# First-layer activations: their low parts subtracted on VectorE instead of on GpSimd

## The chip, the core and the metric

The kernel runs on one core of one Trainium2 chip. The metric is the device time of one launch in microseconds, from the inputs in HBM to the outputs in HBM. Arithmetic is in 32-bit floats. A matrix product of full precision is made of three products in the faster rounded format `fp32r`: each factor is split into a rounded high part and a low part (factor minus high part), and high·high, low·high and high·low are added up.

## The reference

Two blocks of a transformer follow each other, on 2 sequences of 1,024 tokens with 256 features and a context of 154 tokens each:

```
nx       = layernorm(x) * gamma + beta
evidence = softmax(nx Wq (ctx Wk)^T / 16) (ctx Wv)
combined = [nx, evidence, cond]                       # 768 features
probs    = softmax(combined router_W + router_b)      # 3 experts
h_e      = silu(combined e_w1[e] + e_b1[e])           # 512 columns for each of 3 experts
gate     = sigmoid(silu(combined gate_w1 + gate_b1) gate_w2 + gate_b2)
x        = x + gate * (sum_e probs_e (h_e e_w2[e] + e_b2[e]) out_w + out_b)
```

The second block normalizes `x` with a scale and shift from the condition, attends with 16 heads of 16 features to the (modulated) context, projects and adds to `x`.

## The kernel before

**Tiles and units.** The 2,048 tokens are 8 tiles `t` of 256. For each tile the "first layer" (the 256 columns of the gate and the 3 x 512 of the experts, 1,792 in all) is worked off in 7 units `u` of 256 columns. A unit goes through these steps, each a function of its engine's block:

- `za(t,u)` and `z(t,u)` on TensorE (PE in the profile; functions `hidden_first`, `hidden`): two halves of ten products each into one of two PSUM banks (`hidden_banks`).
- `z(t,u)` on ScalarE (ACT; `hidden`): tanh of the bank into the buffer `hidden` (TB).
- `z(t,u)` on VectorE (DVE; `hidden`): (tanh + 1) times the bank, in `hidden`. The PSUM bank is free after it.
- `h(t,u)` on ScalarE (`high`): the rounded copy, into `hidden_high` (SH).
- `h(t,u)` on GpSimd (POOL; `hidden`): `hidden` minus `hidden_high`, into `hidden_low` (SL).
- `p(t,u)` on TensorE (`second`): twelve products of `hidden_high` and `hidden_low` with the second layer's weights into `token_bank`; `evac` on VectorE adds the result, weighted with the expert's probability, to `expert_sum`.

TB, SH and SL have two buffers each, taken in turn, so the tanh of a unit waits until the low part of the unit before the last has been subtracted from TB, and both `h` steps wait for the `p` of the unit before the last.

**The second block of a tile** runs a tile later, between the units of the next one: `res`, `qn`, `shift`, `xhat`, `qx`, `qlow`, `query` make the queries; sixteen `most` steps (TensorE product, then a VectorE reduction over the 308 scores) find the maximum of each head, `row` transposes the maxima, and DMAs from the SP queue (function `row`) put them into the stack of queries; twelve `score` steps (product, exponential on ScalarE) and four `value` steps follow; and then, a tile later again, `raw` (ScalarE), `sum` (GpSimd), `dup`, `sums`, `out` (VectorE), `out` (ScalarE), `outl` (VectorE) and `proj`. `ln`, `norm`, `low`, `att`, `prob`, `route`, `logit` prepare the next tile's inputs and probabilities. `most`, `row` and `score` take three PSUM banks (`score_banks`) in turn: each product waits until the bank's user three before it has been read (`ring_free`).

**What sets the order.** Every engine works off a fixed list. `schedule()` gives each step a slot: tile `t` begins at slot 5 + 14 t, unit `u` at `step` x `u` after that, and each step's offset stands in `PLAN` or, for single tiles, in `PLAN_OF`; steps of one engine are then sorted by slot plus that engine's `DELAY`. The slots only make an order: at run time nothing waits but for semaphores (`wait_ge` with the count from `upto`). Some steps of the next tile have offsets below 14 counted from the tile before it (`ln` to `logit`). `PLAN` has two numbers for steps that the last tile takes in two parts; other tiles use the first one.

## Time and profile before

| | |
|---|---|
| device time, median of 3 runs | 438.0 us (437.63 to 439.25) |
| profiled execution, device time | 439.08 us |
| profiled execution, span on the core | 436.9 us |
| TensorE busy | 422.1 us |
| VectorE busy | 296.3 us |
| ScalarE busy | 223.6 us |
| GpSimd busy | 175.0 us |

The span runs from the first to the last recorded instruction; the device time of the same execution is 2.2 us longer. Busy is time in which an engine has an instruction in hand. A line of the profile names an instruction by its line number in the kernel, the engine, the operation, the output tile, and the input tiles. A helper that emits instructions for several steps has one line for them, as L1688 to L1690 (the three products of a split pair) and L1176 (`split_low`).

### The profile page before, as it was taken

To read this page: it belongs to the slowest core of one execution; us is meant where nothing else is said; L and a number is where in the kernel's file an instruction comes from. 1 tells how busy PE (TensorE), PEld (TensorE's weight loads), DVE (VectorE), ACT (ScalarE), POOL (GpSimd) and SP (SyncE) were. 2 spreads that over 40 slices of the span, in tenths; PEclk is the share of its full clock that TensorE was granted. 3 is DMA by queue.
4 is the path that set the end of the run, shared out by engine and by line. 5 is a ranking of instruction groups with operands and counts; after the bars stand their busy time and mean duration, and the time that the engine had idled before them with its cause. 6 is when DMAs were issued, how large, how long until landed. Compare 5 with 4: busy or idle time off the path is not lost.

```text
span 436.9 us, 9623 instructions
## 1 busy us (share of the span) xinstructions
PE 422.1 (97%) x3629; PEld 384.7 (88%) x3629; DVE 296.3 (68%) x748; ACT 223.6 (51%) x487; POOL 175.0 (40%) x184
## 2 busy tenths in 40 slices
PE   7899999999999999999999999999999899979996
PEld 6578999989998899889998899889988898868876
DVE  2785566674675696739863797389658755891797
ACT  2868643255347543764367246724672356326271
POOL 4545474553353526324523344344433632330020
PEclk9999999999999999999999999999999999998999
DMA  8786102531100210023000300030003021300301
GB/s 288 252 298 269 50 2 47 142 91 31 44 5 1 63 59 30 24 78 116 2 5 13 109 1 5 14 86 0 5 20 80 0 56 28 80 3 26 72 3 48
DMA packets 16837, 27.80 MB, mean 64 GB/s; under 512 B 3800, under 2 KB 9112, under 8 KB 16664
## 3 DMA queue, kind: packets, MB, share of 16 engines
q1 hardware_dynamic: 16664, 27.19, 21.2%
q8 instruction: 29, 0.48, 0.5%
q14 instruction: 16, 0.13, 0.1%
q10 hardware_dynamic: 128, 0.01, 0.0%
HBM read 15.94 MB, written 2.10 MB: 41 GB/s over the span
## 4 chain that ended last, share of the span: by engine, by line
PE 77%; DVE 15%; issue 3%; ACT 3%; DMA 1%; SPq 1%; ACTq 0%
PE hidden_banks L1688 7%; PE hidden_banks L1690 7%; PE hidden_banks L1689 7%; PE score_banks L1695 6%; PE score_banks L2060 5%; PE token_bank L1688 5%; PE token_bank L1689 5%; PE token_bank L1690 5%; PE score_banks L2030 4%; PE value_bank L2083 3%; PE value_bank L2086 3%; PE value_bank L1695 3%; DVE head_maxima L1463 3%; PE hidden_banks L1913 2%; DVE sums L1477 2%
## 5 line engine op out<-in xcount | busy, mean ns | idle before, releaser
L1620 POOL TENSOR_TENSOR hidden_low<-hidden,hidden_high 128x512 fp32r<-128x512 f32 x56 | 72.8, 1300 | 123.5 <-ACT hidden_high L1072 123.4
L1463 DVE TENSOR_REDUCE head_maxima<-score_banks 128x2 f32<-128x308 f32 x128 | 54.6, 473 | 17.1 <-PE score_banks L2030 15.0
L1688 PE MATMUL hidden_banks<-normed_high,hidden_w_high 128*128 128x256 f32 x224 | 64.2, 287 | 0.8 <-issue 0.8
L1689 PE MATMUL hidden_banks<-normed_high,hidden_w_low 128*128 128x256 f32 x224 | 62.5, 279 | 0.0
L1690 PE MATMUL hidden_banks<-normed_low,hidden_w_high 128*128 128x256 f32 x224 | 62.5, 279 | 0.0
L1132 ACT ACTIVATE exp_ring<-score_banks 128x512 f32<-128x512 f32 x96 | 52.6, 600 | 18.8 <-PE score_banks L2060 17.5
L1072 ACT CAST hidden_high<-hidden 128x512 fp32r<-128x512 f32 x56 | 34.8, 622 | 48.2 <-DVE hidden L1380 48.1
L1688 PE MATMUL token_bank<-expert_out_high,hidden_high 128*128 128x256 f32 x192 | 55.7, 290 | 0.0
L1064 ACT ACTIVATE hidden<-hidden_banks 128x512 f32<-128x512 f32 x56 | 33.3, 595 | 41.6 <-PE hidden_banks L1913 40.0
L1690 PE MATMUL token_bank<-expert_out_low,hidden_high 128*128 128x256 f32 x192 | 53.4, 278 | 0.0
L1689 PE MATMUL token_bank<-expert_out_high,hidden_low 128*128 128x256 f32 x192 | 53.4, 278 | 0.0
L1380 DVE SCALAR_TENSOR_TENSOR hidden<-hidden,hidden_banks 128x512 f32<-128x512 f32 x56 | 38.2, 683 | 18.5 <-ACT hidden L1064 18.3
L1688 PEld LDWEIGHTS hidden_banks<-normed_high,hidden_w_high 128*128 128x128 f32 x224 | 42.1, 188 | 2.1 <-issue 2.0
L1689 PEld LDWEIGHTS hidden_banks<-normed_high,hidden_w_low 128*128 128x128 f32 x224 | 42.3, 189 | 0.1
L1690 PEld LDWEIGHTS hidden_banks<-normed_low,hidden_w_high 128*128 128x128 f32 x224 | 42.0, 188 | 0.0
L1688 PEld LDWEIGHTS token_bank<-expert_out_high,hidden_high 128*128 128x128 f32 x192 | 36.2, 188 | 0.5 <-issue 0.2
L1689 PEld LDWEIGHTS token_bank<-expert_out_high,hidden_low 128*128 128x128 f32 x192 | 36.3, 189 | 0.2
L1690 PEld LDWEIGHTS token_bank<-expert_out_low,hidden_high 128*128 128x128 f32 x192 | 36.1, 188 | 0.0
L2030 PE MATMUL score_banks<-pair_keys,query_stack 96*128 96x308 f32 x112 | 29.4, 335 | 2.5 <-DVE head_maxima L1463 1.4
L1913 PE MATMUL hidden_banks<-probs_T_tail,context_w_tail 100*128 100x256 f32 x112 | 31.6, 282 | 0.0
L1689 PE MATMUL hidden_banks<-probs_T_high,context_w_low 128*128 128x256 f32 x112 | 31.2, 279 | 0.0
L1688 PE MATMUL hidden_banks<-probs_T_high,context_w_high 128*128 128x256 f32 x112 | 31.2, 279 | 0.0
(294 smaller groups left out, 1111.5 us busy)
## 6 DMA issues: line engine op xcount, KB each, us to landing
unit_weights<-units SPq DMA_DIRECT2D x7, 768.0 KB, 6.0
query_stack<-queries_high SPq DMA_DIRECT2D x56, 64.0 KB, 2.0
tokens<-x SPq DMA_DIRECT2D x8, 256.0 KB, 3.7
query_stack<-queries_low SPq DMA_DIRECT2D x28, 64.0 KB, 2.0
w_slice<-units SPq DMA_DIRECT2D x7, 256.0 KB, 3.0
out<-tokens SPq DMA_DIRECT2D x7, 256.0 KB, 2.4
w_T<-folds SPq DMA_DIRECT2D x6, 256.0 KB, 6.1
pair_keys<-keys_high SPq DMA_DIRECT2D x16, 77.0 KB
```

The lines of the kernel that those rows point to most:

```text
L1064: nc.scalar.activation(TB[:, ring(t, u), :], Z[:, hidden_bank(t, u), :], ACT.Tanh, scale=0.5).then_inc(scalar_z, 1)
L1072: nc.scalar.copy(SH[:, ring(t, u), :], TB[:, ring(t, u), :]).then_inc(scalar_h, 1)
L1132: nc.scalar.activation(E[:, w % ERING, :], S[:, ring_of[key][0], :], ACT.Exp).then_inc(scalar_score, 1)
L1380: v.scalar_tensor_tensor(out=TB[:, ring(t, u), :], in0=TB[:, ring(t, u), :], scalar=1.0, in1=Z[:, hidden_bank(t, u), :], op0=ALU.add, op1= ...
L1463: v.tensor_reduce(MX[:, s, first:first + step + 1:step], S[:, ring_of[key][0], 0:2 * CTX].rearrange("p (j n) -> p j n", j=2), AX.X, ALU.ma ...
L1620: nc.gpsimd.tensor_tensor(SL[:, ring(t, u), :], TB[:, ring(t, u), :], raw(SH[:, ring(t, u), :]), ALU.subtract).then_inc(gpsimd_h, 1)
L1688: mm(out_, lh, rh, start=start, stop=False, skip_group_check=skip)
L1689: mm(out_, ll, rh, start=False, stop=False, skip_group_check=skip)
L1690: return mm(out_, lh, rl, start=False, stop=stop, skip_group_check=skip)
L1695: last = mm(out_, l, r, start=(i == 0), stop=(i == len(pairs) - 1))
L1913: return mm(half, VWD[0:BROWS, b, c], PTD[0:BROWS, t % 2, :], start=False, stop=True)
L2030: mm(bank, QS[0:STACK, c, P * s:P * s + P], KS[b][0:STACK, c, :, :].rearrange("p j n -> p (j n)"), start=True, stop=True).then_inc(tensor_ ...
```

## The change

The `h` step that makes `hidden_low` moves from GpSimd's list to VectorE's, as a new function `hidden_low` that calls the existing helper `split_low` (a VectorE `tensor_tensor` with subtract). The tanh of ScalarE and `p` of TensorE wait on the new semaphore `vector_h` instead of `gpsimd_h`. All numbers of `PLAN`, `PLAN_OF`, `SETUP` and `DELAY`, from which the orders of the engines' lists come, are set anew. No other instruction is added or removed. The diff, cut to its core:

```diff
--- before.py
+++ after.py
@@ STEPS @@
         "logit": ["l", "s", "prob"],
         "z": ["s"],
+        "h": ["l"],
         "init": ["b"],
...
         "low": ["n"],
-        "h": ["l"],
         "qn": ["rstd"],
@@ DELAY, scalar @@
-        "logit": 1.7, "z": 0.81, "h": 0.3, "gate": 0.4, "qx": 0.4, "query": 0.1, "row": -0.4, "score": 0.2,
-        "out": 1.6, "xhat_last": -0.7, "qx_last": 0.2, "query_last": 0.2, "row_last": 0.5, "score_last": 0,
...
+        "logit": 1.2, "z": 0.9, "h": 0.4, "gate": 0.3, "qx": 0.9, "query": 0.15, "row": -0.2, "score": 0.15,
+        "out": 2.9, "xhat_last": -0.4, "qx_last": 0.3, "query_last": 0.1, "row_last": 0.3, "score_last": 0.1,
@@ DELAY, vector @@
-        "fold": -0.6, "vw": 0.6, "vt": 0.6, "w2": 0.6, "att": 0.2, "route": 0.4, "logit": 1.6, "z": 1, "evac": 0.5,
-        "query": 0, "most": 0.43, "row": 0.4, "proj": 2.5, "last": -0.2, "key": 0.6, "mod": 0.1, "bq": -0.3, "cb": 0,
...
+        "fold": -0.1, "vw": 0.6, "vt": 0.5, "w2": 0.7, "att": 0.1, "route": -0, "logit": 1.3, "z": 0.97, "evac": 0.5,
+        "query": 0.3, "most": 0.45, "row": 0.8, "proj": 2.3, "last": -0.6, "key": 0.4, "mod": -0.1, "bq": 0.7,
...
+        "outl_last": 0.3, "h": 0.6,
@@ DELAY, gpsimd @@
-        "h": 0.6, "ln": 0.86, "qn": -0.2, "low": 0.9, "keyn": 1.2, "split": 2.1,
+        "ln": -0.4, "qn": 0.7, "low": 0.8, "keyn": 3, "split": 1.4,
@@ DELAY, sync @@
-        "query": 13.4, "row": -3.6, "proj": 1.5, "last": -2.1, "key": -0.9, "place": 11.3, "query_last": 3.7,
-        "row_last": -3.6, "stack_last": 1.9,
+        "query": 23.4, "row": -0.7, "proj": 2.7, "last": -3.8, "key": -2.1, "place": 13.3, "query_last": 8.6,
+        "row_last": -12.6, "stack_last": 0.9,
@@ PLAN @@
-    "dup": (37.2, 49.2), "za": -0.4, "step": 1.99, "z": 0.38, "h": 1.5, "p": 3.3, "again": -6.4, "vw": -38.8,
-    "ln": 0.2, "norm": 1.6, "low": 6.6, "att": 7.9, "prob": 9.1, "route": 12.3, "logit": 14.4, "res": 17.4,
-    "qn": 18.4, "shift": 18.5, "xhat": 19.3, "qx": 19.54, "qlow": 20.1, "query": 20.7,
-    "most": (22.11, 22.29, 23.89, 24.92, 26.01, 26.34, 27.35, 28.05), "row": (29.2, 30.6),
...
-    "out": (38.34, 56.69), "outl": (43.37, 97.85), "proj": 43.6, "last": (16, 59.3), "reload": 45.3, "init": 5.2,
+    "dup": (36.83, 44.29), "za": -0.12, "step": 2, "z": 0.45, "h": 1.7, "p": 3.2, "again": -3, "vw": -44, "ln": 6.8,
+    "norm": 1.3, "low": 5.5, "att": 7.7, "prob": 12.7, "route": 12.6, "logit": 14.2, "res": 16.4, "qn": 17.38,
+    "shift": 18, "xhat": 18.42, "qx": 18.7, "qlow": 19.5, "query": 20.4,
+    "most": (22.27, 22.35, 22.87, 23.42, 25.81, 26.78, 27.42, 28.01), "row": (28.65, 36.67),
...
+    "out": (15.7, 77.9), "outl": (42.9, 80.4), "proj": 44.2, "last": (6.5, 80.9), "reload": 55.9, "init": 6.9,
@@ PLAN_OF: it had entries for tiles 0, 1, 3, 5, 6 and 7, and has them for all eight; tiles 2 and 3 @@
+    2: {
+        "norm": 1.6, "value": (34.15, 34.2, 36.28, 36.3), "prob": 8.6, "ln": -0.3, "logit": 16.1, "qx": 18.5,
+        "score": (31.5, 31.7, 32.6, 32.7, 33, 33.3, 34, 34.4, 34.5, 35, 35.3, 35.5), "sums": (37.7, 46),
+        "out": (39.1, 57.1),
+    },
     3: {
-        "vw": 0.9,
+        "proj": 44.3, "logit": 13.8, "qx": 18.4, "ln": -3.8,
+        "score": (32.68, 32.8, 32.9, 33.6, 33.89, 34.23, 34.35, 34.49, 35.23, 35.29, 35.46, 35.56), "vw": 0.94,
+        "value": (35.1, 35.2, 36, 36.3), "norm": 1.8, "query": 20.1, "att": 7.5, "out": (38.5, 58.1), "prob": 7.8,
+        "sums": (37.8, 50.1), "qlow": 19.1, "dup": (37.1, 42.8),
     },
@@ PLAN_OF of tile 6, from which its ln step is placed @@
-        "raw": (34.4, 34.5), "proj": 47.7, "most": (21.9, 22, 24.8, 25.8, 26.5, 27.3, 27.4, 28), "ln": 0.9,
...
+        "most": (21.8, 21.9, 25.1, 25.7, 26.4, 27.1, 27.3, 28.2), "ln": 0.2,
...
@@ scalar, hidden @@
-                    act.wait_ge(gpsimd_h, upto(gpsimd_h, ("h", (g - 2) // NU, (g - 2) % NU), "l"))
+                    act.wait_ge(vector_h, upto(vector_h, ("h", (g - 2) // NU, (g - 2) % NU), "l"))
@@ vector @@
+            def hidden_low(key):
+                t, u = key[1:]
+                g = NU * t + u
+                dve.wait_ge(scalar_h, upto(scalar_h, key, "h"))
+                if g >= 2:
+                    dve.wait_ge(tensor_p, upto(tensor_p, ("p", (g - 2) // NU, (g - 2) % NU), "p"))
+                split_low(SL[:, ring(t, u), :], TB[:, ring(t, u), :], SH[:, ring(t, u), :]).then_inc(vector_h, 1)
@@ gpsimd @@
-            def hidden(key):
-
-                t, u = key[1:]
-                g = NU * t + u
-                pool.wait_ge(scalar_h, upto(scalar_h, key, "h"))
-                if g >= 2:
-                    pool.wait_ge(tensor_p, upto(tensor_p, ("p", (g - 2) // NU, (g - 2) % NU), "p"))
-                nc.gpsimd.tensor_tensor(SL[:, ring(t, u), :], TB[:, ring(t, u), :], raw(SH[:, ring(t, u), :]),
-                                        ALU.subtract).then_inc(gpsimd_h, 1)
@@ tensor, second @@
                 pe.wait_ge(scalar_h, upto(scalar_h, ("h", t, u), "h"))
-                pe.wait_ge(gpsimd_h, upto(gpsimd_h, ("h", t, u), "l"))
+                pe.wait_ge(vector_h, upto(vector_h, ("h", t, u), "l"))
```

## Rows read from the trace of the kernel before

**Rows 1.** The page: busy time of each engine, and the chain that ended last by engine.
```profile
PE 422.1 (97%) x3629; PEld 384.7 (88%) x3629; DVE 296.3 (68%) x748; ACT 223.6 (51%) x487; POOL 175.0 (40%) x184
...
PE 77%; DVE 15%; issue 3%; ACT 3%; DMA 1%; SPq 1%; ACTq 0%
```

**Rows 2.** Waits of TensorE: what waited for whom, us in total, times, longest.
```profile
PE score_banks L2060 <- DMA query_stack<-max_low: 1.7, 1, 1.7
PE score_banks L2030 <- DVE head_maxima L1463: 1.4, 6, 0.3
...
PE score_banks L2030 <- DMA query_stack<-queries_high: 0.9, 1, 0.9
...
PE hidden_banks L1688 <- issue: 0.8, 1, 0.8
...
PE head_bank L1980 <- ACT x_hat L1089: 0.6, 1, 0.6
```

**Rows 3.** Windows from the third maximum on, for six tiles: length, busy time by engine.
```profile
150.04:164.72 14.68, 14.55 (x121) 14.27 (x120) 14.52 (x35) 5.36 (x10) 5.86 (x7) 1.00 0.21 60
196.82:211.50 14.68, 14.68 (x114) 14.27 (x113) 14.13 (x33) 6.51 (x13) 5.04 (x6) 1.00 0.28 84
243.59:258.27 14.68, 14.48 (x120) 14.20 (x119) 14.55 (x34) 5.36 (x10) 5.84 (x7) 1.00 0.20 56
286.97:301.65 14.68, 14.46 (x121) 14.14 (x120) 14.55 (x34) 5.33 (x10) 5.85 (x7) 1.00 0.15 36
330.24:344.92 14.68, 13.69 (x112) 13.17 (x111) 12.90 (x31) 5.43 (x10) 9.27 (x10) 1.00 0.14 35
374.00:388.68 14.68, 13.43 (x104) 12.27 (x103) 14.35 (x32) 4.99 (x9) 6.69 (x9) 1.00 0.13 31
```

**Rows 4.** Groups of instructions: busy us in all, mean ns of one, idle before them.
```profile
L1620 POOL TENSOR_TENSOR hidden_low<-hidden,hidden_high 128x512 fp32r<-128x512 f32 x56 | 72.8, 1300 | 123.5 <-ACT hidden_high L1072 123.4
...
L1429 DVE TENSOR_TENSOR tokens<-expert_sum,tokens 128x512 f32<-128x512 f32 x8 | 5.5, 692 | 0.3
```

**Rows 5.** Timeline of VectorE: start, duration, instruction.
```profile
248.67 0.45 DVE L1496 STREAM_SHUFFLE sums_spread<-sums 128x256 f32<-128x256 f32 x1
...
251.96 0.86 DVE L1463 TENSOR_REDUCE head_maxima<-score_banks 128x2 f32<-128x308 f32 x2
252.73 0.87 DVE L1417 SCALAR_TENSOR_TENSOR expert_sum<-token_bank,router_probs,expert_sum 128x256 f32<-128x256 f32 x2
...
254.29 0.41 DVE L1176 TENSOR_TENSOR probs_T_low<-head_bank,probs_T_high 128x256 fp32r<-128x256 f32 x1
...
258.27 0.74 DVE L1166 BATCH_NORM_STATS2 stats<-tokens 128x6 f32<-128x256 f32 x2
...
259.41 1.28 DVE L1506 SCALAR_TENSOR_TENSOR outs_low<-outs_high,constants,outs_twice 128x1024 fp32r<-128x1024 f32 x1
...
267.42 0.69 DVE L1429 TENSOR_TENSOR tokens<-expert_sum,tokens 128x512 f32<-128x512 f32 x1
268.03 0.68 DVE L1518 TENSOR_TENSOR tokens<-tokens,value_bank 128x512 f32<-128x512 f32 x1
```

**Rows 6.** Timeline of TensorE in the same stretch: `p(4,4)`, a wait, `p(4,5)`, `row(3,0)`.
```profile
249.38 0.28 PE L1688 MATMUL token_bank<-expert_out_high,hidden_high 128*128 128x256 f32 x1
...
252.49 0.41 PE L2030 MATMUL score_banks<-pair_keys,query_stack 96*128 96x308 f32 x1 [0.20 <-DVE head_maxima L1463]
...
254.29 0.28 PE L1688 MATMUL token_bank<-expert_out_high,hidden_high 128*128 128x256 f32 x1
...
259.23 0.39 PE L2039 MATMUL score_banks<-constants,head_maxima 128*16 128x128 f32 x2
```

**Rows 7.** Timeline: four VectorE adds alone, the same beside a GpSimd step, that step.
```profile
227.25 1.80 DVE L1397 SCALAR_TENSOR_TENSOR expert_sum<-expert_bias,router_probs,expert_sum 128x256 f32<-128x256 f32 x4
...
361.00 2.82 DVE L1397 SCALAR_TENSOR_TENSOR expert_sum<-expert_bias,router_probs,expert_sum 128x256 f32<-128x256 f32 x4
...
361.27 1.35 POOL L1620 TENSOR_TENSOR hidden_low<-hidden,hidden_high 128x512 fp32r<-128x512 f32 x1 [2.46 <-ACT hidden_high L1072]
```

More of the change, by code:

```diff
@@ L310 @@
-    7: {
-        "route": 13.2, "most": (19.2, 19.2, 19.3, 19.4, 19.4, 19.6, 20.3, 20.5), "init": 5.6, "sums": (28.4, 36),
-        "za": -0.73, "score": (22.06, 22.59, 22.73, 23.07, 23.16, 23.16, 23.63, 23.73, 24.03, 24.23, 24.34, 24.54),
-        "outl": (33.4, 33.8), "row": (19.96, 21.53), "h": 1.2, "p": 3.5, "last": (39.5, 39.7), "query": 18.06,
-        "xhat": 17.7, "ln": 0.5, "value": (23.2, 23.5, 24.7, 25.8), "proj": 38, "logit": 14.9, "out": (27.3, 33.2),
-        "raw": (23.1, 28.7), "qlow": 18, "qx": 17.62, "dup": (24.9, 28.7), "step": 1.96,
+        "row": (28.6, 36.8),
@@ new lines @@
+        "score": (31.23, 32.12, 32.26, 32.36, 32.85, 33.42, 33.77, 34.21, 34.46, 35.13, 35.28, 36.12),
+        "value": (32.94, 34.35, 36.27, 36.29), "qx": 18.5, "out": (38.5, 64.2), "sum": (34.8, 38), "h": 1.36,
+        "most": (22.27, 22.79, 24.33, 24.75, 25.7, 26.97, 27.6, 28.07), "sums": (37.6, 47.2),
+    },
+    1: {
+        "norm": 1, "p": 3.5, "value": (33.1, 34, 36.2, 36.2), "query": 20.8, "sum": (34.4, 37.3), "prob": 8.4,
+        "ln": -0.1, "score": (31.6, 32.5, 32.6, 32.9, 33.6, 33.6, 34, 34.2, 34.7, 35.4, 35.6, 36.1),
+        "out": (39.3, 63.5), "low": 6.2, "most": (22.28, 22.31, 23.14, 23.27, 25.87, 26.74, 27.32, 28.07),
+        "qlow": 19.3, "logit": 13.4, "qn": 17.7, "sums": (37.7, 47.1),
+    },
@@ new lines @@
+    4: {
+        "prob": 10.2, "most": (22.27, 22.4, 22.9, 23.48, 25.94, 26.78, 27.43, 28.01),
+        "value": (33.97, 34.81, 36.11, 36.12), "sums": (37.3, 48.9), "out": (38.5, 59.6), "query": 20.9,
+        "score": (31.36, 31.82, 32.08, 33.42, 33.42, 33.83, 34.3, 34.52, 34.82, 35.35, 35.54, 35.62), "ln": -0.5,
+        "dup": (36.9, 44.6),
+    },
+    5: {
+        "proj": 43.87, "shift": 18.4, "ln": 0.45, "query": 20.8,
+        "most": (22.4, 22.4, 22.9, 23.4, 26, 26.8, 27.5, 28.1), "value": (32.53, 33.96, 35.56, 35.9), "qlow": 20.7,
+        "prob": 8.29, "score": (31.87, 31.87, 31.94, 32.53, 33.17, 33.5, 34.12, 34.13, 34.17, 35.22, 35.28, 35.44),
+        "out": (38.6, 58.5), "qx": 19.4, "sums": (37.5, 47.4),
+    },
@@ new lines @@
+    6: {
+        "sums": (37.1, 47.1), "prob": 8.5, "stack": (17.1, 18, 23.6, 25.7), "raw": (34.5, 35.2), "logit": 14.97,
+        "out": (37.2, 60.7), "value": (31.9, 31.9, 35.1, 35.6), "att": 7.5, "query": 20.2,
+        "most": (21.8, 21.9, 25.1, 25.7, 26.4, 27.1, 27.3, 28.2), "ln": 0.2,
+        "score": (30.6, 30.7, 30.8, 31.3, 31.4, 31.7, 31.9, 32.1, 32.6, 32.6, 32.8, 32.9), "init": 6.2,
+    },
+    7: {
+        "step": 1.97, "outl": (31.9, 34.9), "xhat": 17.4, "value": (23.4, 23.4, 25.4, 26), "ln": 1.4,
+        "raw": (22.9, 26.6), "h": 1.5, "low": 6.8, "init": 5.9, "query": 18.3, "norm": 3.3, "p": 3.4,
+        "most": (18.9, 19, 19.1, 19.2, 19.3, 19.4, 19.4, 19.6), "prob": 8.7, "qx": 17.7, "dup": (25.5, 28.7),
+        "out": (27.45, 32.07), "res": 16.94,
+        "score": (22.1, 22.2, 22.3, 22.6, 22.8, 23.3, 23.3, 23.5, 23.5, 23.7, 23.9, 24.3), "logit": 14,
+        "sums": (30.5, 33.3), "qlow": 17.4, "row": (20.6, 21.7), "last": (40, 41.5), "proj": 39.6,
```

50 lines of the change are left out of this document (22 added, 28 removed).

## The prediction

> **What bounds the kernel now.** I read the page first, then TensorE's waits, then the windows and timelines of one tile. TensorE has work in hand for 422 of 436.9 us [rows 1]: the reader should see that it is full nearly everywhere, so a change can gain only what TensorE waits, and loses whatever it makes TensorE wait. The named waits from the first `most` on are few [rows 2]: 1.7 us for the DMA of the last row of maxima, 1.4 us for the reductions of `most` in six pieces, 0.9 us for the queries, 0.8 and 0.6 us for single events, 5.4 us together. The rest of the 436.9 - 422.1 = 14.8 us in which it is idle lies in small pieces, in the setup and at the very end.
>
> A mean load of 68% on VectorE hides where it matters. The chain is 15% VectorE [rows 1]. The windows show where it is full: from the third `most` of a tile on, VectorE also makes the division and spreading of the tile before (`dup`, `sums`, `out`). In windows of 14.68 us from that point VectorE is busy for 14.52, 14.13, 14.55, 14.55, 12.90 and 14.35 us [rows 3]. In five of six tiles it is as full as TensorE. GpSimd is busy for 5.0 to 9.3 us in the same windows. Nothing in TensorE's waits names the low parts of the activations: GpSimd stands 123 us waiting to be given them [rows 4]. The step moves from the engine with room to the one that shares the path there.
>
> **The price of one step.** On GpSimd it takes 1300 ns. VectorE has no `hidden_low` before; the same operation on the same shape from SBUF is L1429, 692 ns [rows 4]. Its successor starts 0.61 us after it (268.03 - 267.42) [rows 5], and this is what a step costs a full queue. 56 x 0.61 = 34 us of VectorE's queue (by durations 56 x 0.692 = 39, so 296 to 335 us busy), and 73 us less for GpSimd. The step issues no DMA. The latency of a unit's low part falls by 1300 - 692 = 0.6 us where neither engine queues; TensorE doesn't wait for it now, so I credit that with nothing. Two other things hang on the step: ScalarE's tanh of the unit after the next, and everything behind it in VectorE's list. It waits for ScalarE's rounded copy, so VectorE stands if it is placed too early. The slots put it 0.88 after VectorE's `z` (1.7 + 0.6 against 0.45 + 0.97), some 2.7 us at 14 slots to the 286.97 - 243.59 = 43.4 us of a tile [rows 3], so that wait costs nothing.
>
> **One stretch worked out: the maxima of tile 3.** The new slots (5 + 14 t + offset + delay) give VectorE from `most(3,2)` on: two `most`, `dup`, two `most`, `z(4,4)`, `sums`, two `most`, **`h(4,4)`**, `out`, `z(4,5)`, `evac`, two `most`, **`h(4,5)`**, `route`, two `most`, `z(4,6)`, two `most`, **`ln(6)`**, **`h(4,6)`**, the last two `most`. Before, the same steps stood there without the bold ones (`ln(6)` came after the last `most`), and a 0.08 us reciprocal that now comes earlier. TensorE's list has the same sets of work between the milestones as before, so its times carry over.
>
> - `p(4,4)`: before, all but the third pair of `most` was done at 248.67; that pair costs 252.73 - 251.96 = 0.77. So `h(4,4)` starts at 248.67 + 0.77 - 0.08 = 249.36 and ends at 250.05. TensorE is there at 249.38 [rows 5, 6]: 0.7 us late.
> - `p(4,5)`: VectorE had finished this set at 254.29. Now 254.29 - 0.08 + 0.61 = 254.82, and `h(4,5)` ends at 255.51. TensorE is there at 254.29 - 0.20 (the wait at 252.49 goes, since the pairs of `most` move forward) = 254.09: 1.4 us late.
> - `row(3,0)`: the last `most` ended at 258.27. Added are 3 x 0.61 = 1.83 for `h` and 259.41 - 258.27 = 1.14 for `ln(6)`, less 0.08: 2.89, so 261.16. TensorE is there at 259.23 - 0.20 = 259.03: 2.1 us late.
>
> These lags are measured from the same schedule, so they don't add: TensorE loses 2.1 us here, against 0.2 before. Net 1.9 us.
>
> **The other five stretches.** All get three `h` steps, 1.83 - 0.08 = 1.75 us; only the one above gets `ln` too. Against this stand VectorE's idle time in the window [rows 3] and the lead of the last `most` over `row`, 259.23 - 258.27 = 0.96 us in tile 3 [rows 5, 6], which I take for all. Tiles 1 and 4: idle 0.16 and 0.13, so 1.75 - 0.96 - 0.15 = 0.6 by `row`, and up to the 1.4 of `p(4,5)` by the middle of the stretch; I take 1.0 each. Tile 2: idle 0.55, so 0.2 to 1.4, taken 0.8. Tile 5: idle 1.78, because TensorE came late itself, taken 0.2. Tile 6: here TensorE has little else to do (13.43 of 14.68 us) and the next thing behind VectorE is the 1.7 us DMA wait, so all of it, 1.8. With 1.9 for tile 3 the sum is 1.0 + 0.8 + 1.9 + 1.0 + 0.2 + 1.8 = 6.7 us. Bounds: nothing, if the new order lets VectorE begin earlier by as much; 6 x 2.1 = 12.6 us, if each is like tile 3's.
>
> **The rest.** Of the other waits, 0.9 + 0.8 + 0.6 = 2.3 us [rows 2], the new slots change the surroundings of all; half, 1.2 us, is credited, with 0 and 2.3 as bounds. Setup and tail: VectorE's steps in the tail stand in nearly the same order, and the last `h` lies before them; in the setup the slots of all steps move a little, and nothing in the rows names this step there; 0, with 1 us either way. `init` moves from before `qlow` to before `query`, into idle time of VectorE: 0. `sum` on GpSimd moves later by its slot, but by order only behind `prob`: 0.
>
> Sum against the profiled execution: 439.1 (436.9 of span and 2.2 around it) + 6.7 - 1.2 = 444.6. That execution is 1.1 us above the median of the runs, so 443.5.
>
> **A rule against the step.** An add of four on VectorE, both inputs in SBUF, takes 1.80 us alone and 2.82 us where a GpSimd step that reads SBUF stands beside it [rows 7]; the difference is 1.02 us. The Trainium skill, page "SBUF — State Buffer", section on its two separate sides, says that GpSimd and a VectorE operation with two SBUF inputs take one shared port pair as an exclusive lock for a whole instruction; by that rule, the trace agrees. What it would do here is rival 2.
>
> **Rivals.**
>
> 1. *The order absorbs it (no change).* The new slots pull four pairs of `most` ahead of `sums` and `out`, so the reductions no longer wait behind them; for it speaks that VectorE idles 436.9 - 296.3 = 141 us of the span elsewhere. Against it: the total before `row` is what counts, and it grows. With losses of 0.3 us a stretch: 439.1 + 1.8 - 1.2 = 439.7, so 438.6 beside the median.
> 2. *The lock makes it worse.* Each new step has two SBUF inputs. GpSimd without `hidden_low` still works for 175 - 73 = 102 us, 23% of the span, so some 13 of 56 steps meet one; at up to 1.02 us each in the full stretches (18 steps, 4 meetings) that is 4 us more: 447.5. Against it: its largest user of the port, `hidden_low` itself, has gone from GpSimd.
> 3. *Faster.* GpSimd's step was in the way of `low`, `prob`, `norm` and `sum`, and the freer lists let the new order close TensorE's waits. All 5.4 us of the waits in rows 2 gone gives 438.0 - 5.4 = 432.6; half, the likelier, 435.3. It decides if the load added per stretch falls below the lead of 0.96 us, as by `out` or `ln` done outside it. Against: in rows 3 VectorE has no such room, and these waits name other engines.
>
> **How the numbers follow.** Forecast 0.47, rival 2 0.10, rival 1 0.18, rival 3 0.25. Differences within 0.5% (2.2 us) are about what a measurement of this kernel can tell from no change: slower 0.57, same 0.18, faster 0.25. The range reaches to rival 3's half way less the setup's 1 us, 434.5, and past rival 2's to 448; the forecast's own range is 440.5 to 447.
>
> **What would show it.** `hidden_low` on VectorE at 690 to 700 ns x56 and VectorE near 335 us; GpSimd near 102 us. TensorE's products of `p` (L1688, `token_bank`) waiting for VectorE's `hidden_low` in several tiles, 0.5 to 1.5 us each, and `row` (L2039) waiting for the last reduction; TensorE's busy time unchanged near 422 us, the span longer by the waits alone. I am wrong if the six windows show VectorE full while TensorE doesn't wait (the work before `row` has been cut elsewhere), or if the gain comes from the last tile's wait for the maxima.

## The result, and the profile after

The changed kernel takes 448.4 us in the median (446.76 to 449.32, four runs); the kernel before, run beside it on the same chip, 438.6 us. The ratio is 1.021, with a 95% interval of 1.018 to 1.025. The forecast was 443.5 us and "slower"; the direction is right, the loss is 8 to 10 us instead of 5.5, and the median lies 0.4 us above the upper end of the range. The profiled execution took 446.76 us with a span of 445.0, against 439.08 and 436.9 before: 8.1 us in the spans, and the steps below are read from these.

First the page of the changed kernel: busy time by engine, and the chain that ended last.

```profile
PE 425.7 (96%) x3629; PEld 386.8 (87%) x3629; DVE 324.4 (73%) x804; ACT 222.7 (50%) x487; POOL 104.2 (23%) x128
...
PE 60%; DVE 21%; SPq 6%; issue 5%; ACT 4%; DMA 2%; POOL 0%; POOLq 0%; ACTq 0%; DVEq 0%
```

Against [rows 1] VectorE has 28 us more, GpSimd 71 us less, and VectorE's share of the chain has gone from 15% to 21%. Then the groups of instructions with the moved step, and beside it a step of GpSimd that will matter (busy us in all, mean ns of one, idle before them).

```profile
L1200 DVE TENSOR_TENSOR hidden_low<-hidden,hidden_high 128x512 fp32r<-128x512 f32 x56 | 39.6, 708 | 11.3 <-ACT hidden_high L1096 11.0
...
L1643 POOL TENSOR_TENSOR normed_low<-normed,normed_high 128x512 fp32r<-128x512 f32 x8 | 10.3, 1289 | 40.0 <-ACT normed_high L1052 40.0
```

TensorE's waits (us in total, times, longest), which answer to [rows 2]:

```profile
PE score_banks L2052 <- DVE head_maxima L1495: 4.2, 9, 1.0
PE score_banks L2061 <- DVE head_maxima L1495: 2.5, 5, 1.4
PE token_bank L1710 <- DVE hidden_low L1200: 1.6, 3, 0.5
...
PE score_banks L2052 <- DMA query_stack<-queries_high: 1.1, 2, 0.8
```

Waits for the maxima have grown from 1.4 to 4.2 us, the `row` transposition waits for the last reduction five times, and `p` waits for the low part three times. All of these but two waits of 0.3 us stand in the stretches from a tile's third maximum to its `row`. The windows of 14.68 us from about the third maximum on, as in [rows 3], for tiles 1 to 4 (length, TensorE, its weight loads, VectorE, ScalarE, GpSimd):

```profile
151.43:166.11 14.68, 13.65 (x112) 13.25 (x111) 14.55 (x33) 5.16 (x10) 1.48 (x2) 1.00 0.20 58
200.70:215.38 14.68, 14.68 (x113) 14.21 (x113) 14.55 (x35) 4.69 (x10) 2.48 (x4) 1.00 0.24 63
246.86:261.54 14.68, 13.54 (x110) 13.00 (x109) 14.55 (x33) 5.15 (x10) 2.00 (x3) 1.00 0.14 35
292.60:307.28 14.68, 13.56 (x112) 13.14 (x110) 14.55 (x33) 5.12 (x10) 1.48 (x2) 1.00 0.10 23
```

VectorE is full in all four, as it nearly was before, and in three of them TensorE no longer is: in tile 3, 13.54 against 14.48 us busy, and 110 products against 120 in the same time. That TensorE has lost, and waits for VectorE, is the sign that VectorE has become the bound of this stretch; its own 14.55 us of 14.68 would not show it, since it had nearly as much before. In tiles 5 and 6 the same windows have VectorE at 14.55 and 14.00 us and TensorE at 13.65 and 12.58, against [rows 3] 12.90 and 14.35, 13.69 and 13.43. VectorE's timeline of tile 3, the stretch that the prediction worked out (start, duration), beside [rows 5]:

```profile
246.86 0.86 DVE L1495 TENSOR_REDUCE head_maxima<-score_banks 128x2 f32<-128x308 f32 x2 [0.28 <-PE score_banks L2052]
...
252.62 0.70 DVE L1200 TENSOR_TENSOR hidden_low<-hidden,hidden_high 128x512 fp32r<-128x512 f32 x1
...
258.06 0.69 DVE L1200 TENSOR_TENSOR hidden_low<-hidden,hidden_high 128x512 fp32r<-128x512 f32 x1
258.66 0.42 DVE L1200 TENSOR_TENSOR probs_T_low<-head_bank,probs_T_high 128x256 fp32r<-128x256 f32 x1
...
261.83 0.74 DVE L1190 BATCH_NORM_STATS2 stats<-tokens 128x6 f32<-128x256 f32 x2
...
262.97 0.69 DVE L1200 TENSOR_TENSOR hidden_low<-hidden,hidden_high 128x512 fp32r<-128x512 f32 x1
263.58 0.86 DVE L1495 TENSOR_REDUCE head_maxima<-score_banks 128x2 f32<-128x308 f32 x2
```

And TensorE's, beside [rows 6]: `p(4,4)`, `p(4,5)`, `row(3,0)`, with the wait ahead of each in brackets.

```profile
253.46 0.35 PE L1710 MATMUL token_bank<-expert_out_high,hidden_high 128*128 128x256 f32 x1 [0.52 <-DVE hidden_low L1200]
...
258.85 0.36 PE L1710 MATMUL token_bank<-expert_out_high,hidden_high 128*128 128x256 f32 x1 [0.62 <-issue]
...
264.50 0.39 PE L2061 MATMUL score_banks<-constants,head_maxima 128*16 128x128 f32 x2 [0.42 <-DVE head_maxima L1495]
```

The low part of 252.62 ends at 253.32 and `p` starts at 253.46; the next ends at 258.75 and `p` starts at 258.85, though the trace puts that wait down to "issue"; the last reduction runs until 264.44 and `row` starts at 264.50. From the start of the third maximum to `row` it is 264.50 - 246.86 = 17.6 us, before it was 259.23 - 243.59 = 15.6.

**The whole span in these pieces.** I cut the timeline of each kernel in this way: until the first tile's `row`; the six stretches from the third maximum to `row` of tiles 1 to 6; the six pieces between, from one `row` to the next third maximum; and from the last of these `row` products to the end.

| us, profiled execution | to first `row` | six stretches (each) | six pieces between | after the last | span |
|---|---|---|---|---|---|
| before | 124.1 | 97.0 (16.6 17.9 15.6 15.6 17.2 14.2) | 167.0 | 48.8 | 436.9 |
| after | 124.3 | 103.5 (17.6 18.7 17.6 16.5 16.7 16.3) | 169.8 | 47.4 | 445.0 |

The stretches lost 6.5 us, where the prediction's sum was 6.7; the pieces between lost 2.8 us that it did not have; the end came out 1.4 us shorter.

The pieces do not hold quite the same work in both kernels. Counted by products, TensorE does 748 in the six stretches before and 739 after, and 1,544 and 1,559 in the pieces between. Ten products have moved from just ahead of a `row` to behind it (and one of `z` the other way): six router products (`logit`) in tile 4, and four of `w_slice` in tile 1, which took from 165.65 to 166.60, so 0.95 us. TensorE in tile 4, before:

```profile
302.00 0.17 PE L1900 MATMUL head_bank<-router_context,probs_T_high 128*128 128x8 f32 x1
...
302.58 0.39 PE L2039 MATMUL score_banks<-constants,head_maxima 128*16 128x128 f32 x2
```

and after:

```profile
309.06 0.39 PE L2061 MATMUL score_banks<-constants,head_maxima 128*16 128x128 f32 x2 [0.17 <-DVE head_maxima L1495]
309.20 0.25 PE L1922 MATMUL head_bank<-router_context,probs_T_high 128*128 128x8 f32 x1
```

Six more router products have moved out of the first piece in the same way. With 0.58, 0.95 and 0.59 us put back where they stood, the loss for the same work is 0.8 us up to the first `row`, 8.0 in the stretches (2.0 in tile 1 and 1.5 in tile 4 instead of 1.1 and 0.9), 0.7 in the pieces between, and -1.4 at the end.

### The profile page after: what moved, and what is told of

The parts are those of the page before. It is cut to its first block, busy times and chain, and to the rows that moved or that the text cites. A ratio compares the mean times of both kernels' runs of the same rounds, so it can differ in the third digit from the quotient of the medians.

```text
span 445.0 us, 9623 instructions
## 1 busy us (share of the span) xinstructions
PE 425.7 (96%) x3629; PEld 386.8 (87%) x3629; DVE 324.4 (73%) x804; ACT 222.7 (50%) x487; POOL 104.2 (23%) x128
## 4 chain that ended last, share of the span: by engine, by line
PE 60%; DVE 21%; SPq 6%; issue 5%; ACT 4%; DMA 2%; POOL 0%; POOLq 0%; ACTq 0%; DVEq 0%
DVE head_maxima L1495 6%; PE hidden_banks L1710 5%; PE hidden_banks L1712 5%; PE hidden_banks L1711 5%; PE score_banks L2082 4%; PE score_banks L1717 4%; PE token_bank L1710 4%; PE token_bank L1712 4%; PE token_bank L1711 4%; PE value_bank L2105 3%; PE value_bank L2108 3%; PE score_banks L2052 2%; DVE hidden_low L1200 2%; DVE hidden L1404 2%; SPq L880 2%
## 5 line engine op out<-in xcount | busy, mean ns | idle before, releaser
L1710 PE MATMUL hidden_banks<-normed_high,hidden_w_high 128*128 128x256 f32 x224 | 65.3, 291 | 0.0
L1710 PE MATMUL token_bank<-expert_out_high,hidden_high 128*128 128x256 f32 x192 | 56.6, 295 | 2.6 <-DVE hidden_low L1200 1.6
L1200 DVE TENSOR_TENSOR hidden_low<-hidden,hidden_high 128x512 fp32r<-128x512 f32 x56 | 39.6, 708 | 11.3 <-ACT hidden_high L1096 11.0
L1566 POOL TENSOR_TENSOR rstd<-mean_var,minus_half 128x2 f32<-128x2 f32 x18 | 13.9, 772 | 135.4 <-DVE mean_var L1195 135.4
L1712 PE MATMUL hidden_banks<-probs_T_low,context_w_high 128*128 128x256 f32 x112 | 31.3, 279 | 0.0
```

The source lines that it names most:

```text
L1200: return v.tensor_tensor(dst, full, raw(high), ALU.subtract)
L1710: mm(out_, lh, rh, start=start, stop=False, skip_group_check=skip)
L1712: return mm(out_, lh, rl, start=False, stop=stop, skip_group_check=skip)
```

## The experiments

The kernel before ran beside each and had medians of 438.8 to 439.2 us. "Times" are medians; the pieces are those of the table above.

### 1. The order alone, and the move alone

The first kernel has the changed kernel's slots, but subtracts on GpSimd (delay 0.6, and `sum` at its slots of before). The second has the slots of before, but subtracts on VectorE (delay 0.6). Both kernels have the function `h` on both engines, and one new function says which of them takes a unit:

```diff
+def low_engine(t, u):
+    return "gpsimd"        # first kernel, lists of after
+    return "vector"        # second kernel, lists of before
```

> All slots of the change, but the low parts stay on GpSimd (and its two sums keep their old slots). Theory (the load on VectorE between the third maximum and row costs TensorE its time): about as fast as the kernel before, ratio 0.995 to 1.005, 436 to 441 us, and the six stretches back to within 0.3 us of before. Rival (the new order itself costs the time, wherever the step stands): still 444 to 448 us, ratio 1.015 or more.

> Old slots, the step alone moved to VectorE with its old delay of 0.6 slots. Theory: each stretch gets three steps of 0.61 us against a lead of about 1 us, so slower than before, ratio 1.01 to 1.03, 443 to 451 us. Rival (the new order costs the time): ratio below 1.005. Rival (the new slots are what keeps the loss down): well above the change, over 452 us.

The order alone took 453.4 us (ratio 1.032, 1.029 to 1.035), far from both things that I had expected. The move alone took 459.3 us (1.046, 1.042 to 1.049), as the last of its expectations said. TensorE's largest waits, of the first:

```profile
PE token_bank L1735 <- POOL hidden_low L1667: 4.4, 3, 1.6
PE token_bank L1735 <- issue: 2.6, 4, 1.1
```

and of the second:

```profile
PE score_banks L2053 <- DVE head_maxima L1486: 10.0, 16, 1.6
```

With the old slots the six stretches take 109.5 us, 12.5 more than before, against 6.5 with the new ones, or 8.0 for the same work; so the new slots do take off a good third of the loss there. The first kernel was muddied by its own GpSimd list: `h(4,6)` stood behind `ln`'s reciprocal root, which waits for VectorE, and then took 2.34 us. The timeline of GpSimd:

```profile
265.51 0.70 POOL L1581 TENSOR_TENSOR rstd<-mean_var,minus_half 128x2 f32<-128x2 f32 x1 [3.99 <-DVE mean_var L1210]
266.18 2.34 POOL L1667 TENSOR_TENSOR hidden_low<-hidden,hidden_high 128x512 fp32r<-128x512 f32 x1
```

and of VectorE beside it:

```profile
266.11 1.27 DVE L1553 SCALAR_TENSOR_TENSOR outs_low<-outs_high,constants,outs_twice 128x1024 fp32r<-128x1024 f32 x1
```

### 2. Half of the units on either engine, with the changed kernel's lists

```diff
-    return "vector"
+    return "gpsimd" if u >= 4 else "vector"     # third kernel
+    return "gpsimd" if u < 4 else "vector"      # fourth kernel
```

> The order of the change, with the low parts of units 4, 5 and 6 of every tile (24 steps, those of the full stretches) back on GpSimd and units 0 to 3 (32 steps) on VectorE. Theory: most of the loss is gone, 437 to 441 us, although 32 of 56 steps are still on VectorE. Rival (each step costs alike, by load or by the shared port): 32/56 of the loss stays, about 443 to 444 us.

> The mirror image: units 0 to 3 (32 steps) on GpSimd, units 4, 5 and 6 (24 steps, those of the full stretches) on VectorE. Theory: nearly all of the loss stays, 444 to 448 us. Rival (each step costs alike): 24/56 of the loss stays, about 442 us.

They took 454.3 us (1.033, 1.029 to 1.037) and 452.4 us (1.031, 1.025 to 1.036). Both are slower than the change, both lie outside what theory and rival had expected, and neither decides anything by its total. In the third kernel it is the reason of experiment 1: TensorE waits 4.4 us for GpSimd's low parts, and 2.2 us more that stand under "issue". In the fourth no wait names GpSimd's low parts, but they stand ahead of `ln`'s `rstd` in GpSimd's list, and TensorE waits 1.7 us for `x_hat` and 1.8 us for `tokens` behind it. One reading stands. With only units 4 to 6 on VectorE (24 of 56 steps) five of the six stretches are those of the full change to 0.1 us and the sixth to 0.3 (17.6 18.7 17.6 16.5 16.8 16.0). The mirror image agrees: with only units 0 to 3 on VectorE the stretches are those of the order alone (16.3 19.4 16.3 15.7 16.7 16.9, against 16.3 19.4 16.3 15.6 16.6 17.0). The steps of units 0 to 3 play no part in the stretches.

### 3. The order alone, with `ln` behind

The first kernel again, with GpSimd's delays of before for `qn` and `low`, and 0.3 for `ln` (0.86 before):

```diff
-        "h": 0.6, "ln": -0.4, "qn": 0.7, "low": 0.8, "keyn": 3, "split": 1.4,
+        "h": 0.6, "ln": 0.3, "qn": -0.2, "low": 0.9, "keyn": 3, "split": 1.4,
```

> As the order-only run, with GpSimd's delays for ln (0.3), qn (-0.2) and low (0.9) so that the low part of unit 6 no longer stands behind the small rstd step and ahead of its lock. Theory (in the order-only run TensorE waited for GpSimd's queue, not for anything of the new order): the 4.4 us of waits on GpSimd go, 446 to 449 us. Rival (GpSimd's 1300 ns is too long for the new slots wherever it stands): stays at 452 to 454 us.

It took 448.2 us (1.023, 1.020 to 1.026): 5 us less than the first, so `ln` was a good part of that confusion, and yet as slow as the change with nothing moved to VectorE. The stretches take 101.2 us, the pieces between 172.8. TensorE waits for low parts here too:

```profile
PE token_bank L1735 <- issue: 3.1, 5, 1.1
PE score_banks L2077 <- DVE head_maxima L1510: 2.2, 5, 1.0
...
PE token_bank L1735 <- POOL hidden_low L1667: 1.3, 1, 1.3
```

Each of the five "issue" waits ends 0.10 us after a low part of GpSimd, so they are waits for it too, 4.4 us in all. In the kernel before one `p` waits so, for 0.3 us at 93.35 us, and none in a stretch; in the new lists GpSimd's 1300 ns [rows 4] are too long.

### 4. Load of the same size, in the stretch or outside of it

The kernel before, with 18 unused reductions of 128x512 on VectorE (0.6 us each by the growth of its busy time, 296.3 to 307.1), at the slots of the `h` steps of three units of each tile from the third on:

```diff
+            if t >= 2 and u in (4, 5, 6):     # sixth kernel, in the stretches
+            if t >= 2 and u in (1, 2, 3):     # seventh kernel, outside
+                place(begin + plan(t, "h"), ("extra", t, u))
```

> The kernel before, untouched but for 18 extra reductions of 128x512 (one SBUF input, about 0.68 us each, their result is used by nothing) on VectorE at the old slots of units 4, 5 and 6 of tiles 2 to 7, so three in each full stretch. Nobody waits for them and they share no port. Theory (load in the stretch is what costs): 1.0 to 2.0 us for each of six stretches, 444 to 450 us. Rival (the handing over of the low part, or the shared port, costs): no more than 440 us.

> The same 18 extra reductions at the slots of units 1, 2 and 3 of the same tiles, where VectorE has idle time. Theory: nearly free, within 1.5 us of before. Rival (any work on VectorE costs alike, by its 12 us in all): as slow as the late ones.

In the stretches: 445.2 us (1.018, 1.013 to 1.022). Outside: 439.1 us (1.002, 1.000 to 1.005). Nothing waits for these reductions and they are in nobody's hand-over, so this is load alone. In the stretches they cost 7.1 us (97.0 to 104.15), 0.9 to 1.5 in each, and TensorE waits for maxima eleven times:

```profile
PE score_banks L2038 <- DVE head_maxima L1471: 6.2, 11, 0.8
```

### 5. Other work off VectorE in the stretch

One multiplication of 1.2 us a tile (`out`, 128x1024) goes to GpSimd for tiles 0 to 5, in the changed kernel (with `sum` a little earlier for it) and in the kernel before:

```diff
+            def divide(key):
+                pool.wait_ge(vector_out, upto(vector_out, ("out", t, 0), "o"))
+                nc.gpsimd.tensor_tensor(twice[:, :, :], twice[:, :, :], spread[:, :, :], ALU.mult).then_inc(gpsimd_mul, 1)
```

> The change, with the multiplication of out (128x1024, 1.22 us on VectorE in the middle of each full stretch, about 2.4 us on GpSimd) moved to GpSimd for tiles 0 to 5; the second sum of a tile comes 3 slots earlier in GpSimd's list so that it can. Theory: 1.14 us less in each of six stretches gives back 0.8 to 1.1 us each, 441 to 444 us. Rival (VectorE's load is not what TensorE waits for): 446 to 449 us.

> The kernel before, with the multiplication of the attention's outputs by the reciprocal sums (one operation of 1.2 us on VectorE a tile) on GpSimd for tiles 0 to 5, and the step that waits for it pointed there. If VectorE's load in the six stretches sets their length, 1.2 us less load takes off what its reductions are late there before the change: the kernel before shows 1.4 us of waits for maxima and about a microsecond in front of the last tile, so 435 to 438. If the stretches of the kernel before are bound by TensorE alone, it stays within 0.5% of 438.8.

The change gets 3 us back, less than the 4 to 7 that I had expected: 445.2 (1.016 of the kernel before, 1.013 to 1.019), its stretches 101.7 instead of 103.5. The trace says why. In five of the six stretches a `hidden_low` on VectorE meets the multiplication on GpSimd and takes 1.00 to 1.78 us instead of 0.69, together 3.5 us; in tile 1, VectorE and GpSimd:

```profile
161.42 1.78 DVE L1206 TENSOR_TENSOR hidden_low<-hidden,hidden_high 128x512 fp32r<-128x512 f32 x1
```

```profile
160.25 2.41 POOL L1660 TENSOR_TENSOR outs_twice<-outs_twice,sums_spread 128x1024 f32<-128x1024 f32 x1 [6.04 <-DVE sums_spread L1534]
```

The kernel before, which has no `hidden_low` on VectorE to meet it, becomes faster than both kernels of this case: 436.5 us, ratio 0.995 (0.993 to 0.997). TensorE's waits for maxima fall from 1.4 to 0.6 us. The windows of tiles 1 and 3, beside [rows 3], have VectorE at 13.4 instead of 14.5 us and TensorE a little fuller:

```profile
150.50:165.18 14.68, 14.61 (x120) 14.21 (x120) 13.39 (x33) 5.43 (x10) 8.14 (x8) 1.00 0.22 60
...
243.90:258.58 14.68, 14.60 (x120) 14.17 (x119) 13.43 (x33) 5.41 (x10) 8.15 (x8) 1.00 0.17 47
```

Not all of the gain is that. The span fell by 2.0 us: the stretches gave 1.0, 1.4 came from the end, of which the section on the hardware tells, and the first piece was 0.5 us longer. And the 1.0 us came from tiles 2, 5 and 6. In tiles 1, 3 and 4, where VectorE had been busy for 14.5 of 14.68 us, the stretches stayed as they were with 1.1 us less to do (16.6, 15.7, 15.7, against 16.6, 15.6, 15.6): before the change VectorE was full there, but in time.

### 6. The price of the step varied, in the changed kernel's lists

From the third unit on only half of the columns are subtracted (the low parts of the other half are left out). On VectorE the step then takes 451 ns in the mean instead of 708; on GpSimd, in the kernel of experiment 3, 758 instead of 1294.

```diff
+                n = 256 if g >= 2 else 512
-                split_low(SL[:, ring(t, u), :], TB[:, ring(t, u), :], SH[:, ring(t, u), :]).then_inc(vector_h, 1)
+                split_low(SL[:, ring(t, u), :n], TB[:, ring(t, u), :n], SH[:, ring(t, u), :n]).then_inc(vector_h, 1)
```

> The changed kernel's lists with the low parts on GpSimd, as in the earlier run of that order (448.2), but from the third unit on only the first half of the columns is subtracted (leaves out half of the columns of the low parts), so that the step takes about as long on GpSimd as the whole one takes on VectorE. Theory (VectorE's load in the stretch costs the time, the order only halves it): with neither the load on VectorE nor GpSimd's 1.3 us in the hand-over, 438 to 441. Rival (the new order costs by itself, whoever subtracts): it stays at 446 to 449.

> The changed kernel, with only the first half of the columns subtracted from the third unit on (leaves out half of the columns of the low parts): the same 56 steps in the same lists with the same waits, each about 0.3 us shorter on VectorE. Theory (the load decides): the six stretches hold 3 to 4 of the steps each, so about 1 us less in each of them, and 442 to 445 in all. Rival (the hand-overs or the order decide): within 1 us of the change, 447 to 449.

Half on VectorE: 442.9 us (1.009, 1.007 to 1.012), 5.5 less than the change. Half on GpSimd: 444.5 us (1.012, 1.008 to 1.017); it fell between what theory and rival expected, so both hold a part. The intervals of these two overlap; the pieces of the profiled executions are what they tell. Of the half step on VectorE the profile shows the slowest of four executions (444.56 us), of the change the fastest (446.76), so the spans differ by 2.2 us and the medians by 5.5.

| us | six stretches (each) | pieces between | span |
|---|---|---|---|
| before | 97.0 (16.6 17.9 15.6 15.6 17.2 14.2) | 167.0 | 436.9 |
| new lists, half a step, on GpSimd | 99.4 (16.1 18.9 15.8 15.1 16.5 17.0) | 170.2 | 441.6 |
| new lists, half a step, on VectorE | 101.1 (16.8 18.0 16.8 15.7 16.5 17.3) | 170.0 | 442.8 |
| new lists, the whole step, on VectorE (the change) | 103.5 (17.6 18.7 17.6 16.5 16.7 16.3) | 169.8 | 445.0 |

The stretches grow with VectorE's load, 99.4, 101.1, 103.5; the pieces between do not care about it, 170.2, 170.0, 169.8. All three kernels with the new lists have the moved products, but for one. So in tiles 1, 3 and 4 the load is most or all of the loss: without it 16.1, 15.8 and 15.1 us, against 15.6, 15.6 and 15.0 before for the same work.

Tile 6 has to be read with the clock. In both half-step kernels TensorE's granted clock was at its lower level of 1.2 GHz for 3.4 us inside this stretch (0.50 in the mean from 389.6 to 393.0 us in the one on GpSimd), in the change it was not. VectorE's wait for the products after that unit's `z`, with the half step on GpSimd:

```profile
392.49 0.86 DVE L1510 TENSOR_REDUCE head_maxima<-score_banks 128x2 f32<-128x308 f32 x2 [1.54 <-PE score_banks L2078]
```

and in the change:

```profile
395.33 0.87 DVE L1495 TENSOR_REDUCE head_maxima<-score_banks 128x2 f32<-128x308 f32 x2 [0.26 <-PE score_banks L2052]
```

The difference is 1.3 us (1.53 against 0.26 with the half step on VectorE too). With that estimate taken off, the three sums are 98.1, 99.9 and 103.5, and tile 6 goes from 14.2 over 15.7 to 16.3: 0.6 us for the load and 1.5 for the new lists, in which TensorE waits there for the DMA of the queries (0.83 us in the change), as it did not before.

### 7. The move outside of the stretches, with the old lists

```diff
+    return "vector" if 1 <= u <= 3 else "gpsimd"
```

> The kernel before with its own slots, and only the low parts of units 1, 2 and 3 (24 of 56) on VectorE. Theory (only what is laid into the full stretch costs): VectorE has idle time there, as it had for the 18 added reductions that cost nothing, so 437.5 to 440.5. Rival (every step put in VectorE's list costs by its place in the list, as the move with old slots cost 20 us for 56): 24/56 of 20, so 446 to 449.

It took 445.2 us (1.013, 1.011 to 1.016): the theory's 437.5 to 440.5 fails as a total, and the time lies 0.8 us under the rival's 446 to 449. Its stretches are those of the kernel before to 0.1 us (16.6 17.9 15.6 15.6 17.1 14.2, against 17.2 in tile 5), as the theory has it. But the first `row` comes at 129.3 instead of 124.1, and the pieces between take 169.8 instead of 167.0. One reason stands in the timelines, of VectorE:

```profile
106.10 0.88 DVE L1478 SCALAR_TENSOR_TENSOR queries_low<-head_bank,query_bias,queries_high 128x256 fp32r<-128x256 f32 x2 [2.48 <-ACT queries_high L1125]
106.89 1.57 DVE L1191 TENSOR_TENSOR hidden_low<-hidden,hidden_high 128x512 fp32r<-128x512 f32 x1
```

of GpSimd:

```profile
106.65 1.26 POOL L1634 TENSOR_TENSOR normed_low<-normed,normed_high 128x512 fp32r<-128x512 f32 x1 [8.49 <-ACT normed_high L1043]
```

and of TensorE:

```profile
108.61 0.36 PE L1711 MATMUL token_bank<-expert_out_high,hidden_high 128*128 128x256 f32 x1 [2.24 <-DVE hidden_low L1191]
```

The low part stood behind a step that itself waited 2.48 us for ScalarE, then took 1.57 us beside GpSimd's `normed_low`, and `p` came 2.24 us late. VectorE's idle time is idle because it waits in order; a step that others wait for and that stands behind such a wait is late with it. The reductions of experiment 4, for which nobody waits, cost 0.5 us in the pieces between (167.5); none of them stood as early as this one, since they begin with tile 2.

The rest can be told apart by the starts of `hidden_high`, of which every kernel has 56. The first comes 1.6 us later than before (35.4 against 33.8), and the ninth still 1.5 (98.0 against 96.5). So 1.6 of the 5.2 us come from the setup, where the granted clock was 0.50 from 11.5 to 18.2 us in this execution and full in that of the kernel before (whether that is all of the 1.6 us is open), and 3.6 us from the units around the wait shown. The 2.8 us between have a name too:

```profile
PE value_bank L2106 <- ACT exp_ring L1147: 2.4, 3, 1.0
```

In one of these waits (0.98 us, until 237.77) ScalarE had stood 1.42 us at its rounded copy, because VectorE was late with `z`, and the exponential that TensorE needed stood behind that copy in ScalarE's list.

In the move alone of experiment 1 the same two pieces lose nearly the same: until the first `row` +4.5 us there and +5.2 here, between +3.9 and +2.8. The +12.5 in the stretches are what the units 4 to 6 add; of them nothing is here.

## Why the prediction was right, and where it was off

- **VectorE as the bound of the stretch: right.** The load outside costs 0.2% and inside 1.8% (experiment 4), and stretches grow with the price of the step (experiment 6). It was not yet the bound before: 1.1 us less of it left tiles 1, 3 and 4 as they were (experiment 5). The prediction's "in five of six tiles it is as full as TensorE" is generous, since in tile 2 it has 14.13 against 14.68 us [rows 3].
- **Tile 3, worked out step by step: right.** The order on VectorE is the one worked out. Predicted were lags of 0.7, 1.4 and 2.1 us; the waits shown are 0.52, 0.62 and 0.42, so lags of 0.5, 1.1 and 1.6, and the stretch grew by 2.0, against 1.9. It holds the same 127 products in both kernels, as the prediction had assumed. What the named waits lack is probably in short stalls that count as busy (last section).
- **The other five stretches: the sum is near, with luck in it.** Predicted 1.0, 0.8, 1.0, 0.2, 1.8 for tiles 1, 2, 4, 5, 6; measured 1.1, 0.8, 0.9, -0.4, 2.1. With tile 3 it is 6.5 against 6.7. But the assumption that TensorE's sets of work stay the same fails in tiles 1 and 4: for the same work they lost 2.0 and 1.5, and the sum is 8.0. And I had put all of it down to VectorE's queue. The queue's share is 103.5 - 99.4 = 4.1 us as measured, 5.4 with the low clock's 1.3 us taken out; the other 2.6 belong to the new lists. For tile 6 the size was right and the reason mostly wrong.
- **"The rest": here the prediction failed.** The step credited 1.2 us for other waits that the new slots would change, with 0 and 2.3 as bounds. Those waits did shrink by as much: of the three, 0.8 and 0.6 us are gone and the 0.9 for the queries has become 1.1 (the 0.8 stood in tile 5's stretch, which is why that one got shorter). But the new lists have losses of their own. Outside of the stretches the pieces came out at +0.2, +2.8 and -1.4 us, so +1.6; for the same work it is +0.8, +0.7 and -1.4, so +0.1, and the -1.4 is no merit of the change (last section). I had bounded this term by the waits of the kernel before, as if a new order could only take waits away; its bounds should have had a side above nothing. With the pieces as measured the sum is 439.1 + 6.5 + 1.6 = 447.2, and the execution took 446.8.
- **From the execution to the median: a larger miss than that of the sum.** The prediction took 1.1 us off because its profiled execution lay so far above the median. The changed kernel's profiled execution is the fastest of four and lies 1.6 us below it. Of the 4.9 us between 443.5 and 448.4, 2.2 are in the sum (444.6 against 446.8) and 2.7 in this step, which rests on the spread of the executions and not on the change.
- **The latency credit: nothing, and rightly so for the old order, but for one wait of 0.3 us.** What I didn't see is that the new lists leave the hand-over less time. In them the difference between 1294 and 758 ns on GpSimd is worth 446.2 - 441.6 = 4.6 us of span (experiments 3 and 6).
- **Rival 2, the lock: the mechanism is there, its weight small.** Two of 56 steps met a GpSimd step instead of 13, at 1.37 and 1.21 us instead of 0.69. Together 1.2 us of VectorE's time, and neither stands in a stretch.
- **Rival 1, the order absorbs it: half true.** With the old slots the span is 456.3 us and with the new ones 445.0, against 436.9 before: they take back 11.3 of 19.4 us.
- **Rival 3, faster: no.** The wait for the last maxima's DMA did vanish, but nothing was gained by it (last section).
- **The signs.** `hidden_low` at 690 to 700 ns: 54 of 56 took 0.65 to 0.70, the mean is 708. GpSimd near 102: 104.2. VectorE near 335: 324.4, since the records overlap those on both sides, and a step adds 28.1 / 56 = 0.50 us to the busy time. `p` and `row` waiting: yes. TensorE's busy time unchanged near 422: no, 425.7.

What stays open: how the new lists lose 2.6 us in the stretches, beside the wait for the queries in tile 6, and 1.5 us up to the first `row` and between. Single waits of that size are not named there. What the timelines have is more products whose successor starts about 0.1 us late after a change of step (`hidden_low` behind `hidden_high` of `p` 21 times against 9, the second product of `z` 14 against 3), and as many in the kernel of half a step on GpSimd; it is about 2.3 us by these two kinds, and about 1.3 us when the kinds that became fewer are counted too, from 125 us on. No experiment took it away.

## What to carry to other kernels

Before moving a step to another engine, read that engine's load in the stretch where the path touches it: VectorE's mean was 68%, and the same load cost 1.2 us a tile in one place and nothing in the other. Then ask who waits for the moved step and what stands ahead of it in the list that it joins; an engine that idles because it waits in order has no room for work that others wait for. If all slots are set anew with the change, that is a second change: give it a term with both signs, and time it apart. And before two kernels are compared piece by piece, count the products in each piece.
